# Two graph convolutions with a gate and a layer norm on one core: other engines for logits, row sums and squares, other places for evacuations, split items and loads

## The reference

```python
def _gcn_layer(x, adj, W, b):
    d_inv_sqrt = (jnp.sum(adj, axis=1) + 1e-09) ** (-0.5)
    msg = d_inv_sqrt[:, None] * adj * d_inv_sqrt[None, :] @ x
    return jax.nn.relu(msg @ W + b)
H_f = _gcn_layer(feature_x, adj, W_f, b_f)
H_s = _gcn_layer(spatial_x, adj, W_s, b_s)
attn = jax.nn.sigmoid(jnp.concatenate([H_f, H_s], axis=1) @ W_att + b_att)
y = x + attn * H_f + (1.0 - attn) * H_s          # x is feature_x
out = (y - mean(y)) / sqrt(var(y) + 1e-05)       # over the 128 features
```

## Time and profile before

| | |
|---|---|
| median of 3 runs | 422.5 us (422.21 to 422.69) |
| the profiled execution | 422.08 us |
| its span, first to last instruction | 420.0 us |
| PE busy | 374.0 us (89%) |
| PEld busy | 308.0 us (73%) |
| DVE busy | 291.8 us (69%) |
| ACT busy | 285.4 us (68%) |
| POOL busy | 171.1 us (41%) |
| mean granted PE clock | 0.976 of full |

### The profile page before, as it was taken

One profiled execution on the slowest core, in us unless ns is written; L12 is line 12 of the kernel. 1 busy time (PEld: TensorE's weight loads), 2 busy tenths in 40 slices (PEclk: granted clock), 3 DMA queues, 4 the chain that ended last, 5 costly groups with the idle time before them and its releaser, 6 DMA issues.

```text
span 420.0 us, 5140 instructions
## 1 busy us (share of the span) xinstructions
PE 374.0 (89%) x1680; PEld 308.0 (73%) x1680; DVE 291.8 (69%) x377; ACT 285.4 (68%) x338; POOL 171.1 (41%) x222
## 2 busy tenths in 40 slices
PE   0779998699969999999899989999999999988950
PEld 0567887488758887888688868888888888867740
DVE  2579983596466966597646966488656669398895
ACT  3768588887888749887888597674533672657545
POOL 1103001021000881068101999150001947889975
PEclk9999999999989999999999999999999999998985
DMA  8999999999999999999999999897655353240002
GB/s 311 388 424 424 417 421 420 422 421 420 421 423 421 414 343 423 424 422 419 421 421 421 411 417 385 313 374 275 226 185 183 137 179 123 101 151 27 25 26 75
DMA packets 25529, 132.84 MB, mean 316 GB/s; under 512 B 2848, under 2 KB 7712, under 8 KB 11296
## 3 DMA queue, kind: packets, MB, share of 16 engines
q1 hardware_dynamic: 25504, 132.53, 78.9%
HBM read 130.42 MB, written 2.10 MB: 316 GB/s over the span
## 4 chain that ended last, share of the span: by engine, by line
DMA 31%; PE 30%; POOL 16%; ACT 8%; DVE 7%; issue 5%; SPq 1%; POOLq 0%; DVEq 0%; ACTq 0%
DMA nat<-in_adj 18%; DMA raw<-in_At 13%; PE sums L352 10%; PE sums L353 10%; PE sums L354 10%; POOL S L678 6%; ACT Ah L537 4%; ACT nat L550 4%; POOL fin L689 3%; DVE Al L417 3%; POOL fin L684 2%; POOL xs L685 2%; POOL vare L694 2%; DVE xs L467 1%; POOL rstd L697 1%
## 5 line engine op out<-in xcount | busy, mean ns | idle before, releaser
L352 PE MATMUL sums<-Ah,Yh 128*128 128x512 f32 x512 | 202.5, 395 | 26.8 <-DVE Yl L428 18.1
L417 DVE TENSOR_TENSOR Al<-raw,Ah 128x2048 fp32r<-128x2048 f32 (+1 forms) x70 | 152.3, 2180 | 99.8 <-ACT Ah L537 99.6
L354 PE MATMUL sums<-Al,Yh 128*128 128x512 f32 x512 | 200.8, 392 | 0.0
L353 PE MATMUL sums<-Ah,Yl 128*128 128x512 f32 x512 | 200.7, 392 | 0.0
L537 ACT ACTIVATE Ah<-raw 128x2048 fp32r<-128x2048 f32 (+1 forms) x70 | 123.4, 1768 | 59.8 <-PE sums L354 28.6
L352 PEld LDWEIGHTS sums<-Ah,Yh 128*128 128x128 f32 x512 | 97.1, 190 | 50.5 <-DVE Yl L428 19.3
L550 ACT ACTIVATE nat<-nat 128x2048 f32<-128x2048 f32 x53 | 101.6, 1916 | 18.8 <-DMA nat<-in_adj 17.5
L354 PEld LDWEIGHTS sums<-Al,Yh 128*128 128x128 f32 x512 | 96.9, 189 | 20.5
L353 PEld LDWEIGHTS sums<-Ah,Yl 128*128 128x128 f32 x512 | 97.0, 190 | 19.7
L440 DVE TENSOR_TENSOR acc<-sums,acc 128x512 f32<-128x512 f32 x112 | 71.3, 680 | 6.7 <-PE sums L354 6.7
L643 POOL TENSOR_SCALAR dg<-rs 128x1 f32<-128x1 f32 x22 | 14.2, 644 | 150.3 <-ACT nat L550 150.0
(11 more groups left out here) (40 smaller groups left out, 130.9 us busy)
## 6 DMA issues: line engine op xcount, KB each, us to landing
raw<-in_At SPq DMA_DIRECT2D x63, 1024.0 KB, 10.1
nat<-in_adj SPq DMA_DIRECT2D x56, 1024.0 KB, 11.5
xs<-in_xs SPq DMA_DIRECT2D x7, 512.0 KB, 11.2
out<-xs SPq DMA_DIRECT2D x32, 64.0 KB, 1.6
raw<-in_At SPq DMA_DIRECT2D x4, 256.0 KB, 10.3
xs<-in_xs SPq DMA_DIRECT2D x1, 384.0 KB, 9.2
xs<-in_xs SPq DMA_DIRECT2D x1, 128.0 KB, 2.4
watt<-in_W_att SPq DMA_DIRECT2D x1, 128.0 KB, 10.2
```

The costliest lines, as they stand in the source:

```text
L352: pe.matmul(to, Yh[:, t % YRING, hs], high, start=first, stop=False)
L353: pe.matmul(to, Yl[:, t % YRING, hs], high, start=False, stop=False)
L354: mm = pe.matmul(to, Yh[:, t % YRING, hs], low, start=False, stop=last)
L417: dve.tensor_tensor(Al[:, k % SPLITS, a * IB:b * IB], raw[:, k % RAWS, a * IB:b * IB], Ah[:, k % SPLITS, a * IB:b * IB], ALU.subtract).the ...
```

## The change

- **Pieces.** The first 18 items are split in four pieces instead of the first two, on ScalarE, on VectorE and in PE's waits. The Yh and Yl of an item's tiles are made behind the first piece (for an item that isn't split, behind the whole). 
- **Evacuations.** Up to item 47 all runs that ended with item k - 2 are evacuated ahead of `low(k)`. At items 2 and 6 the first two runs that ended with item k - 1 are evacuated too.
- **Loads.** Row load 4 goes ahead of the raw load of item 3; the load of the first tile of x goes behind the first two row loads.
- **Logits.** All 32 are made by one VectorE instruction with its accumulator (`logit`), ahead of `low(k)`; POOL's product with watt and ScalarE's sum are gone.
- **Statistics.** For the first 28 tiles VectorE's `join` gives the row sum of y through its accumulator, POOL makes minus the mean of it (`mean`), ScalarE takes the squares of y minus the mean and sums them (`square`), and POOL makes the variance of that. The last four tiles keep BN_STATS and BN_AGGR, now in `statistics`.
- **Lags.** Logits and joins come at lag 5 (before 6 and 7), squares at 6, normalisations at 7 (before 9); the steps behind the loop are in another order.

```diff
...
+PIECED = 18
...
 def plan(T):
...
-    for k, r in [(0, 0), (1, 1), (4, 2), (5, 3), (8, 4), (9, 5), (10, 6), (11, 7)]:
+    for k, r in [(0, 0), (1, 1), (5, 3), (8, 4), (9, 5), (10, 6), (11, 7)]:
...
+    parts[3], parts[4] = [4], [5]
...
-    L_MIX, L_LOGIT, L_JOIN, L_NORM = 4, 6, 7, 9
+    L_MIX, L_JOIN, L_SQUARE, L_NORM = 4, 5, 6, 7
...
-    BY_DVE = T - 2 * GT
...
     def group_at(k, lag):
...
         def pieces(k):
-            return [(i, i + 1) for i in range(GT)] if k < 2 else [(0, GT)]
+            return [(i, i + 1) for i in range(GT)] if k < PIECED else [(0, GT)]
...
         def nat_here(eng, n):
...
             def load_x(m):
...
-            sp.dma_start(xs[:, 0:1, :], xs_v[0, :, 0:1, :]).then_inc(x_first, 16)
             for k in range(K):
...
+                if k == 0:
+                    sp.dma_start(xs[:, 0:1, :], xs_v[0, :, 0:1, :]).then_inc(x_first, 16)
...
                 if k == FINAL:
...
-                if k >= 2:
+                if k >= PIECED:
...
-                    if k < 2 and half == 0:
+                    if k < PIECED and half == 0:
...
-                    if k < 2 and a == 0:
-                        y_low(k)
+                    if a == 0:
+                        for r in y_at[k]:
+                            y_low(r)
...
             def y_low(r):
...
-            def own_logit(r):
+            def logit(r):
...
-                                         accum_out=lg[:, r:r + 1]).then_inc(dlogit_ok, 1)
+                                         accum_out=lg[:, r:r + 1]).then_inc(logit_ok, 1)
...
             def join(r):
...
-                                         in1=xs[:, r, 0:F], op0=ALU.mult, op1=ALU.add).then_inc(y_ok, 1)
+                                         in1=xs[:, r, 0:F], op0=ALU.mult, op1=ALU.add,
+                                         accum_out=ysum[:, r:r + 1]).then_inc(y_ok, 1)
+            def statistics(r):
...
-                if r >= 1:
-                    dve.wait_ge(aggr_ok, r)
+                if r > T - GT:
+                    dve.wait_ge(aggr_ok, r - (T - GT))
...
-                dve.wait_ge(stats_ok, r + 1)
+                dve.wait_ge(stats_ok, r - (T - GT) + 1)
...
             def of_group(g):
...
+            evacuated = set()
+            def evacuate_new(runs_ended):
+                for e in runs_ended:
+                    if e not in evacuated:
+                        evacuated.add(e)
+                        evacuate(e)
             for k in range(K):
...
-                while ended and k < 2 * G:
-                    evacuate(ended.pop(0))
-                if len(ended) == GT:
-                    evacuate(ended.pop(0))
+                if k < FINAL:
+                    evacuate_new(ended)
+                if k < G:
+                    evacuate_new([e for e in evac_order if end_item[e] == k - 1][:2 if k % GT == 2 else 0])
...
+                g = group_at(k, L_JOIN)
+                if g is not None:
+                    for r in of_group(g):
+                        logit(r)
                 low(k)
-                for r in y_at[k]:
-                    if r >= 2:
-                        y_low(r)
+                if g is not None:
+                    for r in of_group(g):
+                        join(r)
                 g = group_at(k, L_MIX)
...
-                for e in ended:
-                    evacuate(e)
-                g = group_at(k, L_JOIN)
-                if g is not None:
-                    for r in of_group(g):
-                        join(r)
-            for r in of_group(TAIL - 3):
+                evacuate_new(ended)
+            for r in of_group(TAIL - 2):
+                logit(r)
+            for r in of_group(TAIL - 2):
...
-            for r in of_group(TAIL - 2):
+            for r in of_group(TAIL - 1):
+                logit(r)
+            for r in of_group(TAIL - 1):
...
-            for r in of_group(TAIL - 1):
-                own_logit(r)
...
-            join(BY_DVE)
-            for i, r in enumerate(of_group(TAIL)):
+            for r in of_group(TAIL):
...
-                if i == 1:
-                    join(r - GT)
-            join(T - GT - 2)
-            join(T - GT - 1)
-            for r in of_group(TAIL):
-                own_logit(r)
-            for r in of_group(TAIL):
-                join(r)
+            for rows in PAIRS:
+                for r in rows:
+                    logit(r)
+            for rows in PAIRS:
+                for r in rows:
+                    join(r)
+                for r in rows:
+                    statistics(r)
...
         @block.scalar
...
-                    if k < 2 and a == 0:
-                        y_high(k)
+                    if a == 0:
+                        if k == COLLECT + 3:
+                            column_sums()
+                        for r in y_at[k]:
+                            y_high(r)
...
             def row_sum(n):
...
-            def logits(r):
-                act.wait_ge(hw_ok, r + 1)
-                act.activation(fin[:, r % ROWS, H_ALL], fin[:, r % ROWS, H_ALL], ACT.Copy,
-                               accum_out=lg[:, r:r + 1]).then_inc(logit_ok, 1)
             def gate(rows):
...
-                if a < BY_DVE:
-                    act.wait_ge(logit_ok, b)
-                else:
-                    act.wait_ge(dlogit_ok, b - BY_DVE)
+                act.wait_ge(logit_ok, b)
...
+            def square(r):
+                act.wait_ge(less_ok, r + 1)
+                act.activation(fin[:, r % ROWS, H_F], xs[:, r, 0:F], ACT.Square, bias=less[:, r:r + 1],
+                               accum_out=ysq[:, r:r + 1]).then_inc(ysq_ok, 1)
...
             def normalise(r):
...
                 high(k)
-                if k == COLLECT + 3:
-                    column_sums()
-                for r in y_at[k]:
-                    if r >= 2:
-                        y_high(r)
                 if k == FINAL:
...
-                g = group_at(k, L_LOGIT)
+                g = group_at(k, L_JOIN)
...
-                    for r in of_group(g):
-                        logits(r)
...
                 g = group_at(k, L_NORM)
...
+                g = group_at(k, L_SQUARE)
+                if g is not None:
+                    for r in of_group(g):
+                        square(r)
                 g = group_at(k, L_MIX)
...
-            for r in of_group(TAIL - 4):
+            for r in of_group(TAIL - 3):
...
-            for r in of_group(TAIL - 2):
-                logits(r)
...
-            for r in of_group(TAIL - 3):
+            for r in of_group(TAIL - 2):
+                square(r)
+            gate(of_group(TAIL - 1))
+            for r in of_group(TAIL - 2):
...
-            gate(of_group(TAIL - 1))
+            for r in of_group(TAIL - 1):
+                square(r)
...
-            for r in of_group(TAIL - 2):
-                normalise(r)
...
-                pool.tensor_tensor(less[:, a:b], rs[:, a:b, 0], rs[:, a:b, 1], ALU.add).then_inc(less_ok, b - a)
-                pool.wait_ge(less_ok, b - FULL)
-                pool.tensor_tensor(dg[:, a:b], less[:, a:b], tiny[:, 0:b - a], ALU.add).then_inc(dg_ok, b - a)
+                pool.tensor_tensor(dsum[:, a - FULL:b - FULL], rs[:, a:b, 0], rs[:, a:b, 1],
+                                   ALU.add).then_inc(dsum_ok, b - a)
+                pool.wait_ge(dsum_ok, b - FULL)
+                pool.tensor_tensor(dg[:, a:b], dsum[:, a - FULL:b - FULL], tiny[:, 0:b - a],
+                                   ALU.add).then_inc(dg_ok, b - a)
...
-                if r < BY_DVE:
-                    pool.wait_ge(dif_ok, r + 1)
-                    pool.wait_ge(res_ok, r + 1)
-                    pool.tensor_tensor(f[:, H_ALL], f[:, H_ALL], watt[:, :], ALU.mult).then_inc(hw_ok, 1)
+            def mean(rows):
+                a, b = rows[0], rows[-1] + 1
+                if a < T - GT:
+                    pool.wait_ge(y_ok, b)
+                    pool.tensor_tensor(less[:, a:b], ysum[:, a:b], share[:, 0:b - a], ALU.mult).then_inc(less_ok, b - a)
+                else:
+                    pool.wait_ge(aggr_ok, b - (T - GT))
+                    pool.tensor_tensor(less[:, a:b], zero[:, 0:b - a], mv[:, a:b, 0],
+                                       ALU.subtract).then_inc(less_ok, b - a)
...
             def deviation(rows):
...
-                pool.wait_ge(aggr_ok, b)
-                pool.tensor_tensor(vare[:, a:b], mv[:, a:b, 1], epsc[:, 0:b - a], ALU.add).then_inc(vare_ok, b - a)
-                pool.tensor_tensor(less[:, a:b], zero[:, 0:b - a], mv[:, a:b, 0], ALU.subtract).then_inc(less_ok, b - a)
+                if a < T - GT:
+                    pool.wait_ge(ysq_ok, b)
+                    pool.tensor_scalar(vare[:, a:b], ysq[:, a:b], 1.0 / F, 1e-5, ALU.mult,
+                                       ALU.add).then_inc(vare_ok, b - a)
+                else:
```

(19 more changed lines are left out.)

8 lines of the change are left out of this document (6 added, 2 removed).

## The result

The changed kernel took 424.12 us (median of 13 runs) beside 422.5 us for the kernel before (13 runs); the ratio is 1.0036, with a 95% interval of 1.0024 to 1.0049. Measured again together with the first experiments it was 423.94 us beside 423.19, a ratio of 1.0021 (1.0005 to 1.0036). So it is slower by 0.2 to 0.4%, 1 to 1.5 us. One of its 13 runs, the one that was profiled first, ran at a granted clock of 0.755 and took 487.45 us; it is left out of the ratio and of every reading, and all rows "of after" are from a further execution (423.08 us, span 421.3 us, clock 0.973).

The account below looks back on a forecast made before the run. It took PE and the full DMA queues to bound the first two thirds, PE's gaps the rest. 422.1 + 3.2 (evacuations) - 1.7 (tail), plus 0.4 to the median, less 0.3 (front): 423.7 us, range 418.3 to 426.5.

Parts of the forecast that it names:

- the likeliest case: POOL's additions meet a fourth low part and the loop takes most of POOL's relief: 422.2 to 425.5 us, chance 0.42.
- Front gain: Pieces, early evacuations, load order: PE some 5 us ahead at item 18, lost by items 40 and 44; 0 to -0.4 us.
- Moved evacuations: Items 21, 29, 37: evacuations ahead of low parts push these onto POOL's work; +3.2 us, bounds 0 and +4.5.
- What was carried on: Item 21: POOL ends 2.0 to 2.9 us later, queued transfers give most back, 0.7 us carried on.
- The 1.3 us of half clock: Item 40: a PE gap of 3 to 4 us; a similar earlier gap was followed by about 1.3 us at half clock.
- The tail: Last third: POOL's relief against a new serial loop with logits beside mixes; -1.7 us, bounds -4.5 and +1.
- The serial loop: Last third, across ScalarE, VectorE and POOL: 13.3 us a group where PE needs 12.6; contention 0.5 us a group.
- with it 0.8 and 0: With logits contending with mixes, the last product comes 0.8 us nearer the first and the end 0 us earlier.
- without the contention: Were logits not to slow mixes, the last product would start 4.9 us nearer the first, the end 4.5 us earlier.
- rival C: Last third: each logit locks POOL for its whole 0.41 us, 7.4 us instead of 3; 427 to 429 us, chance 0.12.
- B: Items 21 and 37: meetings of low parts and POOL's additions don't matter; 418 to 421 us, say 419.8, chance 0.36.
- D: Whole kernel: the change doesn't do what it says, low parts late at items 16 to 20, edits cancel; 422 to 423, chance 0.10.

Follow-up runs that it names:

- e3: The changed kernel with the front of before (2 items in pieces, old evacuation rule and load order), so the tail part alone: 420.5 us, ratio 0.9939 to before.
- e4: The changed kernel, but at items 21, 29 and 37 only the first of four ended runs is evacuated ahead of the low part: 420.63 us, ratio 0.9935 to before.
- e7: e4 with items 2 to 17 split as a whole again instead of in pieces: 420.4 us, ratio 0.9945 to before.
- e6: The changed kernel, but at item 37 only the first of four ended runs is evacuated ahead of the low part: 420.8 us, ratio 0.9957 to before.
- e2: The kernel before with the front part alone (18 items in pieces, evacuations ahead of low parts, load order): 426.32 us, ratio 1.0082 to before.
- e9: e3 with each logit reading only 128 of its 256 columns: 416.3 us, ratio 0.9838 to before.
- e5: The kernel before with one edit, all four runs evacuated ahead of the low part at items 21, 29 and 37: 425.92 us, ratio 1.0097 to before.
- e8: e4 with the last run evacuated after two logits of group 6, last relus ahead of squares, group 7 mixed ahead of group 6's deviation: 417.57 us, ratio 0.9862.
- e11: e8 with each group's normalisation one item later on ScalarE, behind the next item's high part: 413.61 us, ratio 0.9782 to before.
- e10: The changed kernel with POOL's four additions to S for item 38 cut to 64 of 512 columns: 421.05 us, ratio 0.9953 to before.

## Why the prediction was right, point by point

Forecast 423.7 us, measured 424.12 and 423.94: the likeliest case came in. Against before that is 1.2 us forecast and 1.5 and 0.9 measured. By the times of the two halves the terms were 0.3 and 0.9 us off, in opposite directions: the front 3.5 us (2.5 to 4.5) for 3.2, the tail -2.6 (-1.8 to -3.4) for -1.7. By the profiles of before and after they were closer: 2.99 us behind at item 52, and from there to the end of the span 98.9 us instead of 100.6, a gain of 1.7. Of the 0.9 us between the two ways of reading the tail, 0.3 lie outside the span (execution less span is 2.1 us in before, 1.8 in after and e3); for the rest, the profiled execution of before, 422.08 us, is faster than its median in any comparison.

**Front gain, counted as nothing (0.3 us in the sum): right, but for part of its working.** PE was to start item 18 near 122 (122.42), to be 5 us ahead there (4.9), and to have lost it by item 40. The times show it: with all of the front but the three places 420.6 (e4), without the pieces 420.4 (e7), without any of it 420.5 (e3). The prediction had the pieces share in the 5 us at item 18; e7 has 4.7 of them without pieces. And items 40 and 44 were given as the places where the gain is lost, but it doesn't reach them: in e4 2.7 us are left at item 26 and 0.2 at item 36. The raw loads, which land at the same time with and without the lead, took it at item 18; that they also did so from item 26 to 36 is likely but was not tested.

**Moved evacuations, +3.2 us: right in mechanism, place and size.** The front alone measured +0.82%, 3.5 us, and putting the three back 3.3 (e4). At item 21, against the earlier trace rows, DVE and POOL in after:

```profile
132.53 4.87 DVE L447 TENSOR_TENSOR acc<-sums,acc 128x512 f32<-128x512 f32 x8
137.32 2.28 DVE L423 TENSOR_TENSOR Al<-raw,Ah 128x2048 fp32r<-128x2048 f32 x1
...
137.35 2.41 POOL L658 TENSOR_SCALAR dg<-rs 128x1 f32<-128x1 f32 x1 [8.99 <-ACT nat L571]
...
140.38 16.94 POOL L695 TENSOR_TENSOR S<-S,raw 128x512 f32<-128x512 f32 x8
```

The low part was foreseen at 137.3. It was the degree that it hit, 2.41 us instead of 0.34, not an addition; the eight additions took 16.94 us, as long as before. POOL ended 2.1 us later (2.0 to 2.9 foreseen). What was carried on, 0.7 foreseen, is 0.8 us at item 40 by e6 against e4 and 0.5 by their times, both too small to be told from nothing. At item 37 I had the low part end at 232.8 (233.90) and POOL's first addition 2.0 us later than 230.74. It started only 1.35 later, 230.74 against 232.09, when its data landed, but then ran into two low parts, and the four took 9.24 us instead of 7.48. Together D came 3.0 us later, and item 40 at 253.53 (253 foreseen), item 44 at 277.19 (277). The 1.3 us of half clock that I held possible did not come in after, but did in e2; see below.

**The tail, -1.7 us: right in mechanism, too small at both ends.** e3 measured -0.61%, 2.6 us, the profiles 1.7. The wait of 6.91 us at item 60's low part in the earlier trace rows is gone. The last product started 85.0 us behind the first (82 to 87 foreseen; before it was 87.4 by the chain and 87.55 by the timeline). The serial loop was put at 13.3 us a group and is 13.6, and its contention at 0.5 a group, which is what three POOL operations at 0.63 to 0.65 us instead of 0.45 come to. The step that was mis-sized is "with it 0.8 and 0": with the contention the last product came 2.6 us nearer to the first, and the end 1.7. The other end was too small as well: "without the contention" the product was to come 4.9 us nearer and the end 4.5, and e9, with only part of the contention gone, has 6.6 and is 6.9 us below before. That -1.7 fits is therefore in part luck: it was a choice between two ends that both gave some 1.7 us too little. The last product's length, which the prediction held fixed at the 2.59 us of the earlier trace rows, works both ways: 3.62 and 3.78 in after and e3 ate some 1 us of the gain, and 2.05 in e9 gave 0.5.

**The Trainium skill's rule on the logits.** By the Trainium skill, page "SBUF — State Buffer", section "SBUF: two separate sides", a logit would hold POOL for its whole length, and rival C would have been near. The runs decide against that for this instruction: an addition beside a 0.56 us logit took 0.63 us instead of 0.45, and beside one half as long 0.50. Where the two engines meet again and again, in after, both advance by 0.60 us an instruction:

```profile
363.77 0.67 DVE L466 SCALAR_TENSOR_TENSOR fin<-fin,watt 128x256 f32<-128x256 f32 x1
364.37 0.67 DVE L466 SCALAR_TENSOR_TENSOR fin<-fin,watt 128x256 f32<-128x256 f32 x1
...
363.52 0.64 POOL L702 TENSOR_TENSOR xs<-xs,fin 128x128 f32<-128x128 f32 x1
364.12 0.64 POOL L701 TENSOR_TENSOR fin<-fin 128x128 f32<-128x128 f32 x1
```

Undisturbed, POOL takes 0.42 us from start to start (362.25, 362.67, 363.09) and a logit 0.35 (365.49, then the low part at 365.84). If one stood still while the other ran, a pair would need 0.77. For the low part, also a VectorE operation with two operands in SBUF, the trace agrees with the Trainium skill: a degree of 0.34 us took 2.41 beside a low part of 2.28, a shift of 0.20 took 1.26 until the low part ended.

**The rivals.** B (the meetings do not matter; decided by item 40 at 250.6) is out: 253.53, and e5. It describes e4 and e6, which take the meeting away, well: 420.6 and 420.8 for 419.8. C is out by the tail's gain, and a row of mixes takes 0.98 us on the mean of a group (375.03 to 378.95), under the 1.1 set. D is out: e2 and e3 show two effects that nearly cancel, but not that nothing happens; items 16 to 18 came 2.5 to 6 us earlier.

What I did not see beforehand is that the tail had 7 us more in it: the order of the last evacuation (e8) and the normalisation in front of the high part (e11). The prediction names both ("ScalarE's high part of item k+1 now waits behind the normalisation of the group before", "evacuation 63 stands behind the logits and joins of group 6") as costs of the change.

## What to carry to other kernels

Where a step is moved ahead of another on an engine, look not at that engine, which may have time, but at what the displaced step now overlaps on its neighbour: here eight evacuations cost PE nothing on VectorE's side (e10), and a low part that began 2.8 us later (231.62 beside 228.83 in e6), inside POOL's additions, cost 3 us. A serial loop over three engines that is 0.9 us a group longer than the bound engine's work shows no gap for many groups and then sets the end; compare periods, not gaps. Before the order of a tail is taken as given, ask of each instruction that a wait names whether its place in the program or its data holds it.
